# A fused layer pair on one core: half 0's choice moved behind the index scores, rotary products held for them, and only a quarter of the input rows prepared ahead of attention

## What is computed

```python
x = x + attention(layernorm(x))     # top-32 index mask, rotary Q and K
x = x + mixture0(layernorm(x))      # rms_norm, 8 experts, top 2
x = x + state_space(layernorm(x))
x = mixture1(layernorm(x)) + x      # 8 experts, top 2, and a shared one
```

```python
index_scores = sum_h relu(iq_h @ ik) * iw_h          # 4 heads
mask = top-32 of index_scores in each row
attn = softmax(rope(Q) @ rope(K) * scale + mask) @ V
...
scores = rms_norm(x) @ w_router
ids = top_k(scores, 2); c = softmax(scores)[ids]
out = sum over the 2 chosen experts of c * expert(x)
```

## Time and profile before

| | us |
|---|---|
| three runs | 1346.49 to 1353.12, median 1350.16 |
| the profiled execution | 1351.29 |
| its span in the trace | 1349.5 |
| VectorE busy in it | 945.9 (70%) |
| TensorE busy in it | 1057.1 (78%) |
| start until ScalarE's first normalised tile | 16.47 |
| attention | 16.47 to 251.3 |
| first expert tile on TensorE | 285.74 |

### The profile page before, as it was taken

The page is one execution under the profiler, slowest core; times in us unless marked ns, Lnnn a source line. Parts: engine busy times, 40 slices in busy tenths (PEclk is TensorE's granted clock), DMA queues, the critical chain, the costliest instruction groups (busy, mean ns, idle before and its releaser), DMA issues. The chain is left out here.

```text
span 1349.5 us, 20293 instructions
## 1 busy us (share of the span) xinstructions
PE 1057.1 (78%) x4202; PEld 615.6 (46%) x4203; DVE 945.9 (70%) x2283; ACT 746.9 (55%) x1826; POOL 834.6 (62%) x602
## 2 busy tenths in 40 slices
PE   3888867449999955888989888897784229999995
PEld 3666745327777831333333333333223215555563
DVE  4999899633333333799999999989997715455573
ACT  3767746235555547858586776756531115555542
POOL 1433248447517557877886888788782577437276
PEclk9999879569999976999999999899898559999998
DMA  8994002226524425343434354443540026435335
GB/s 244 160 148 138 1 8 24 18 35 88 81 57 88 85 33 111 86 143 131 156 115 169 124 157 124 135 160 115 184 143 0 32 57 94 83 74 95 79 67 103
DMA packets 140460, 133.22 MB, mean 99 GB/s; under 512 B 14579, under 2 KB 121699, under 8 KB 140259
## 3 DMA queue, kind: packets, MB, share of 16 engines
q1 hardware_dynamic: 107106, 115.55, 32.2%
q0 software_dynamic: 33280, 16.86, 11.2%
HBM read 98.66 MB, written 31.60 MB: 97 GB/s over the span
## 5 line engine op out<-in xcount | busy, mean ns | idle before, releaser
L1740 POOL TENSOR_TENSOR ss_HC<-ss_Hs,ss_Cb 128x512 f32<-128x512 f32 x256 | 317.6, 1270 | 91.7 <-PE ss_Y L1514 70.7
L1514 PE MATMUL ss_Y<-ss_HC,g_ident 128*128 128x512 f32 x512 | 267.8, 641 | 46.4 <-POOL ss_HC L1740 38.8
L1809 DVE TENSOR_TENSOR_SCAN ss_Hs<-ss_dA,ss_dBu 128x512 f32<-128x512 f32 x256 | 297.2, 1203 | 6.3 <-ACT ss_dA L1656 6.0
L827 POOL DMA_INDIRECT rows<-m_XS,g_slot x128 | 181.3, 1417 | 69.2 <-issue 35.8
L1127 PE MATMUL m_x_UP<-g_m_w,m_x_gT 128*128 (+1 forms) x532 | 204.5, 491 | 6.7 <-issue 2.6
L1656 ACT ACTIVATE ss_dA<-ss_delta,g_A 128x510 f32<-128x510 f32 x256 | 167.7, 712 | 56.9 <-DVE ss_Hs L1809 56.7
L1514 PEld LDWEIGHTS ss_Y<-ss_HC,g_ident 128*128 128x128 f32 x512 | 90.2, 197 | 207.1 <-POOL ss_HC L1740 148.1
L1801 DVE TENSOR_TENSOR ss_dBu<-ss_duP,ss_Bb 128x512 f32<-128x512 f32 x256 | 163.4, 685 | 21.0 <-DMA ss_Bb<-bc_rows 16.7
L1147 PEld LDWEIGHTS m_x_DP<-g_m_w,m_x_hT 128*128 128x128 f32 (+1 forms) x908 | 131.5, 190 | 80.0 <-issue 38.3
L1147 PE MATMUL m_x_DP<-g_m_w,m_x_hT 128*128 (+3 forms) x908 | 161.7, 296 | 5.3 <-ACT m_x_hT L1214 3.1
L1107 POOL DMA_INDIRECT g_X<-out_rows,g_slot x64 | 99.3, 1551 | 80.1 <-DMA out_rows<-m_x_YO 57.5
(11 more groups left out here) (266 smaller groups left out, 1826.5 us busy)
## 6 DMA issues: line engine op xcount, KB each, us to landing
ss_Bb<-bc_rows SPq DMA_DIRECT2D x64, 512.0 KB, 4.9
ss_Cb<-bc_rows SPq DMA_DIRECT2D x64, 512.0 KB, 4.0
rows<-g_Z SPq DMA_DIRECT2D x2, 5031.0 KB, 55.3
m_x_G<-rows SPq DMA_DIRECT2D x156, 64.5 KB
out_rows<-m_x_YO SPq DMA_DIRECT2D x156, 64.0 KB
g_m_w<-in_w_up SPq DMA_DIRECT2D x1, 2816.0 KB, 10.2
g_m_b<-in_b SPq DMA_DIRECT2D x1, 2160.0 KB, 11.5
g_X<-in_x SPq DMA_DIRECT2D x4, 512.0 KB, 5.7
```

The lines of the kernel that those rows point to most:

```text
L827: self.nc.gpsimd.indirect_dma_start(self.XG, bass.IndirectOffsetOnAxis(self.rt.slot[k][:, t:t + 1], 0), self.XS[:, t, :], None, compute_op ...
L1514: ins = nc.tensor.matmul(Yp[:, h, :], ident[:], HC[n % 2][:, h, :], start=False, stop=n == N - 1)
L1740: nc.gpsimd.tensor_tensor(HC[n % 2][:, h, :], Hs[n % 4][:, h, :], Cb[g % 2][:, n % 2, :], ALU.mult).then_inc(hc_ready.sem, 1)
L1809: v_.tensor_tensor_scan(Hs[n % 4][:, h, :], dA[n % NA][:, h, :, :].rearrange("p s t -> p (s t)"), dBu[:, h, :], 0.0, ALU.mult, ALU.add).th ...
```

## The change

1. *Input rows.* `InputRows` takes the place of `row_stats`. Ahead of attention only the first quarter (8 tiles) gets moments and scales, and the constants are loaded right behind the first quarter of X. The other 24 tiles' moments open VectorE's program in attention, their root is in ScalarE's step 0, their scales at the end of VectorE's step 1. ScalarE's normalising for sequence 4 waits for them.
2. *Statistics for the mixture.* BN_STATS of the updated tiles stands behind round 1 of `choose`, the variance behind round 2, and the `Chain` wait after the statistics goes.
3. *Step 12.* `vector_choose` stands behind index scores, round 0 and update; round 1 and 2 follow, then `vector_slots`, then round 3. `vector_tables` goes to the experts' block, first on VectorE; TensorE waits for it there.
4. *GpSimd from step 12 on.* The bias addition of sequence s (and so the rotary products behind it in GpSimd's program) waits for the index scores of s-1.
5. *Second choice.* The reweighting and the first 4 of its 16 scatters stand at the end of GpSimd's program in attention; 12 stay in the experts' block.

```diff
-def row_stats(nc, tag, chain, shifted, rooted, X, mean, scales, eps2, loads=None, x_loaded=(), shift=None):
+class InputRows:
...
+    def vector_moments(self, dve, lo, hi):
+        v, link = self.nc.vector, Chain(dve, self.chain)
+        n = T // len(self.loaded)
+        for t in range(lo, hi):
+            if t % n == 0:
+                dve.wait_ge(self.loaded[t // n], 16)
+            ins = v.bn_stats(self.st[:, t, :], self.X[:, t * D:(t + 1) * D])
...
+def first_rows(nc, rows, hi, loads):
...
+            rows.vector_moments(dve, 0, hi)
+            rows.vector_scales(dve, 0, 0, hi)
...
                 def normalise(s, v):
+                    if s == early // 2:
+                        act.wait_ge(rows.scaled.sem, rows.scaled.after(1))
...
+                    if s == 0:
+                        rows.scalar_root(act, 1, early, T)
...
                     u = 1 - v
-                    if s == LAST:
-                        dve.wait_ge(d.s.scalar_kept.sem, d.s.scalar_kept.after(1))
-                        d.vector_choose(dve, 0)
                     if middle:
                         index_scores(s - 1, u)
                         choose(s - 1, u, range(0, 1))
                     if tail and s >= 3:
                         update(s - 3, u)
-                        if s - 3 < HT // 2:
-                            dve.wait_ge(x_updated.sem, x_updated.after(s - 3))
-                            d.vector_stats(dve, 2 * (s - 3), 2 * (s - 2))
-                        if s - 3 in (GS - 1, 2 * GS - 1):
-                            b = (s - 3) // GS
-                            d.vector_variance(dve, b * d.G, (b + 1) * d.G)
+                    if s == LAST:
+                        dve.wait_ge(d.s.scalar_kept.sem, d.s.scalar_kept.after(1))
+                        d.vector_choose(dve, 0)
                     if middle:
                         choose(s - 1, u, range(1, 2))
+                    if 3 <= s < 3 + HT // 2:
+                        dve.wait_ge(x_updated.sem, x_updated.after(s - 3))
+                        d.vector_stats(dve, 2 * (s - 3), 2 * (s - 2))
+                    if middle:
+                        choose(s - 1, u, range(2, 3))
+                    if s - 3 in (GS - 1, 2 * GS - 1):
+                        b = (s - 3) // GS
+                        d.vector_variance(dve, GS * (b + 1) - 1, b * d.G, (b + 1) * d.G)
                     if s == LAST:
                         d.vector_slots(dve, 0)
-                        d.vector_tables(dve, 0)
                     if middle:
-                        choose(s - 1, u, range(2, TOPK // 8))
+                        choose(s - 1, u, range(3, TOPK // 8))
+                    if s == 1:
+                        rows.vector_scales(dve, 1, early, T)
...
+                rows.vector_moments(dve, early, T)
                 steps(dve, step)
...
+                        if s >= LAST:
+                            pool.wait_ge(idx.sem, idx.after(s - 1))
+                            pool.sem_inc(skipped, 1)
                         x = X[:, ds(s * W2, W2)].rearrange("p (t d) -> p t d", d=D)
...
                 steps(pool, step)
+                d.pool_reweight(pool, 0, 1)
+                d.pool_scatter(pool, 1, 0, HT // 4, ALU.add)
...
-        Chain(dve, self.chain)(ins)
+        ins.then_inc(self.s.stated.sem, 1)
...
                 if inside:
-                    d.pool_reweight(pool, 0, 1)
-                    d.pool_scatter(pool, 1, 0, HT, ALU.add)
+                    d.pool_scatter(pool, 1, HT // 4, HT, ALU.add)
...
                         d.tensor_score(pe, d.HG + g, g * d.G)
+                    pe.wait_ge(d.s.tabled.sem, d.s.tabled.after(0))
...
                 if inside:
+                    d.vector_tables(dve, 0)
                     d.vector_stats(dve, HT, T)
...
             def first_loads(sp):
-                n = T // len(x_loaded)
-                for t in range(0, T, n):
-                    sp.dma_start(X[:, t * D:(t + n) * D].rearrange("p (t d) -> p t d", d=D), xd[:, t:t + n, :]).then_inc(x_loaded[t // n], 16)
-                for dst, src in first:
-                    sp.dma_start(dst, src).then_inc(first_loaded.sem, 16)
+                for q in range(len(rows.loaded)):
+                    sp.dma_start(X[:, q * early * D:(q + 1) * early * D].rearrange("p (t d) -> p t d", d=D),
+                                 xd[:, q * early:(q + 1) * early, :]).then_inc(rows.loaded[q], 16)
+                    if q == 0:
+                        for dst, src in first:
+                            sp.dma_start(dst, src).then_inc(first_loaded.sem, 16)
```

More of the change, by code:

```diff
@@ L139, in attention, with _ @@
+def first_rows(nc, rows, hi, loads):
+    with nc.Block() as block:
+        @block.sync
+        def _(sp):
+            loads(sp)
+        @block.vector
+        def _(dve):
+            rows.vector_moments(dve, 0, hi)
+            rows.vector_scales(dve, 0, 0, hi)
+        @block.scalar
+        def _(act):
+            rows.scalar_root(act, 0, 0, hi)
+def attention(nc, rows, early, d, zeroed, X, shift, scales, ident, w, bias, b_iw, b_o, rope, loads, clear):
     with ExitStack() as ctx:
@@ L1909, in later_loads @@
                     sp.dma_start(dst, src).then_inc(w1.loaded.sem, 16)
[L1911 removed]
+            first_rows(nc, rows, early, first_loads)
             wait_loaded(nc, first_loaded, len(first))
[L1913 removed]
+            attention(nc, rows, early, d0, zeroed, X, shift, scales, ident, w, bias, b_iw, b_o, rope, later_loads, clear)
         experts(nc, "m0_x_", tile_signals, d0, True, X, XS0, rt, XG0, Y0, None, HT, w0, True, ident)
```

86 lines of the change are left out of this document (35 added, 51 removed).

## The result

The changed kernel takes 1329.97 us (median of 4 runs, 1327.85 to 1335.7) against 1351.43 of the kernel before (1346.49 to 1353.12): ratio 0.9854, 95% interval 0.9813 to 0.9895. I had said 1326, within 1319 to 1336. The profiled execution has a span of 1327.7 against 1349.5 us, 21.8 less.

The account below looks back on a forecast made before the run. VectorE was taken to bound attention, GpSimd's second-choice scatters the gap behind it, then TensorE the expert stage. 4.0 + 3.3 + 3.0 + 6.7 + 7.5 = 24.5 off 1351.3 gave 1326.8, stated as 1326, range 1319 to 1336.

Parts of the forecast that it names:

- The start, 4.0: Ahead of attention: starting with 8 tiles' statistics gains 5.4 us, less 1.4 for six scales in step 1: 4.0.
- The statistics, 3.3: Updated tiles' statistics in attention: 7 x 0.35 us from their new place plus 0.8 for the two variances: 3.3.
- Step 12, 3.0: Attention step 12: 1.9 us from waits, 1.2 from tables, 3.1 from blocking, less 3.2 for the choice blocked: 3.0.
- the 6.2: Upper figure for step 12's gain in us, if nothing blocks the choice, as the scans suggested.
- Steps 13 to 15, 6.7: Attention steps 13 to 15: held GpSimd work leaves the index scores, 7.2 us less 0.5 for a relu wait: 6.7.
- Second choice, 7.5: Gap before the first expert tile: four scatters and the copy's wait leave it, 8.0 us less 0.3 and 0.2: 7.5.
- The sum: Whole kernel: the five terms together take 24.5 us off the profiled execution's 1351.3, giving 1326.8.
- the choice isn't blocked: Rival for step 12: GpSimd does not block the choice, 3.2 us more gain, 1323; chance 0.12.
- Another engine becomes the bound: Rival in attention: TensorE's and ScalarE's round takes half of 3.3 + 3.0 + 6.7, 1333; chance 0.12.
- The moved scatters come late: Rival at attention's end: scatters stretch or GpSimd still scatters when VectorE is through; 7.5 shrinks to about 1, 1333; chance 0.05.
- The start: Rival ahead of attention: SyncE's issue or barrier takes as long, or moments reach into at_IW; 4.0 lost, 1330; chance 0.06.
- slower, by the clock: Rival in the expert stage: 125 us of it at granted clock 0.80 instead of 1.00, ending above 1357; chance 0.03.

Follow-up runs that it names:

- d_start_back: Changed kernel with all 32 tiles' statistics and scales, and all of X loaded, ahead of attention again; at_IW of step 1 at 38.01 against 33.31 us.
- a4_hold_rotary: Changed kernel with GpSimd's rotary product of step 12 held until the choice has weighed; at_IW of step 12 22.88 us behind step 11's instead of 24.86.
- e_best: Changed kernel with step 12's rotary product held, bias additions of steps 14 and 15 in GpSimd's wait, five scatters moved instead of four; 1323.65 us, ratio 0.9805.
- a1_no_hold: Changed kernel without GpSimd's wait for the index scores ahead of the bias addition from step 12 on; 1325.91 us.
- c_old_place_free: Changed kernel without GpSimd's hold and with slots and tables where they stood before; 1326.41 us.
- b_scatters_back: Changed kernel with the copy and all 16 scatters of the second choice in the experts' block; first scatter to first tile 89.05 us.
- e_change_again: The changed kernel itself, unaltered, measured and profiled a second time; 1329.46 us.

## Why the prediction was right, and where its steps were not

- **The start, 4.0:** 4.66 measured, and d_start_back gives it back. Attention started 0.66 earlier than I put it, since SyncE was through at 9.60 and not at 10.4. Of the spare time that I put at 3.8 us, 1.94 went to the wait for X and 1.3 to the stretched TENSOR_SCALAR, which my sum left out; 0.56 remained.
- **The statistics, 3.3:** 2.80 by step 11 in the profile, 2.27 in the second. In the plain step 0.40 each (11.43 against 11.83) instead of 0.35, which made 3.41 by step 9. Step 10 gave nothing: VectorE waits 1.03 for ScalarE's root in it, as I feared, and it took 18.35 us against 17.74. It took 16.13 to 18.41 in the kernels that are the same up to there, so the term's size is known only within 2 us.
- **Step 12, 3.0:** 3.89 measured (24.86 us against 28.75). The mechanism was right and its price near: 2.32 - 0.29 + 1.00 - 0.29 = 2.74 for the 3.2 that I took. The waits gave 2.4 (3.23 less 0.87) instead of 1.9. The Trainium skill ("SBUF — State Buffer", section "Who interferes with whom") gave that side of the bound, and here the trace agrees. The other side, that nothing is blocked, rested on a misreading: the scans of the earlier trace rows do not read two SBUF tensors. ss_dBu, their second input, lies in PSUM in this kernel, so they say nothing against the rule, and the 6.2 had no row behind it. The one scan that does read two SBUF tensors beside GpSimd, in a4_hold_rotary and e_best, was slowed (0.86 instead of 0.41).
- **Steps 13 to 15, 6.7: this step failed.** The words were "Held GpSimd work leaves them". The scores did become 2.46 everywhere, but the hold has no part in it (a1_no_hold). The slots' new place has one: without it and without the hold the scores of steps 13 and 14 lose 1.8 us again. The other 5.4 of the 7.2 are gone without either (c_old_place_free), and what freed them stays open. I priced the hold and did not work out where GpSimd's scatters would stand. Nor did all 7.2 us reach the first tile. By at_IW of step 15 4.95 more us had been gained since step 12 (16.30 against 11.35), and 6.59 in the second profile, whose step 15 was not lengthened by the lower clock (last section). From there to its end in attention VectorE takes longer than before (20.21 us against 18.67), so that 3.41 are left of the 6.7, and 5.37 in the second profile.
- **Second choice, 7.5:** 7.74 from the opening of the block to the first tile (26.37 against 34.11), and 5.6 to 7.0 by b_scatters_back, which counts the later opening too. I had said GpSimd's last scatter and VectorE's end would be within 1 us. VectorE ended 2.36 us behind its end, and yet the block waited for GpSimd: 3.54 us pass there behind the last scatter, which no row of before shows, since GpSimd had long been idle at that change of block.
- **The sum:** 24.5 became 22.25 at the first tile and 21.8 in the span. VectorE's end fell from 251.32 to 236.56; before, and then in the second profile of the change:

```profile
250.71 0.61 DVE L452 SCALAR_TENSOR_TENSOR g_X<-at_b,at_rinv,g_X 128x128 f32<-128x128 f32 x2 [3.83 <-PE at_b L308]
251.63 3.19 DVE L646 BATCH_NORM_STATS2 m_d_st<-g_X 128x6 f32<-128x128 f32 x16 [0.32 <-PEq L214]
```

```profile
237.43 0.47 DVE L828 TENSOR_TENSOR m_d_cmp<-m_d_end,g_tile_of_half 1x312 f32<-1x312 f32 x1 [1.41 <-PEq L223]
```

These 14.76 us are 4.66 + 2.80 + 3.89 + 3.41, where I had 4.0 + 3.3 + 3.0 + 6.7 = 17.0. At the change of block 0.24 are lost to GpSimd (idle 0.56 instead of 0.32), and 1.1 in the second profile; then come the 7.74. So the total came within 10% partly by luck: the start and step 12 gave 1.6 more than I put, steps 13 to 15 3.3 less. And GpSimd took over by no more than 0.2 to 1.1 us; the kernel with six scatters shows that the terms don't add beyond that. The last part passed one to one, within the 5 us by which that stretch varies anyway. The range's lower end was wrong by its own terms: 1326.8 less 3.2, 1.6 and 1.1 is 1320.9, not 1319.
- **The rivals:** "the choice isn't blocked" fell by the 2.32 and 1.00 us rows. "Another engine becomes the bound" was half true, with GpSimd in the place of TensorE and ScalarE. "The moved scatters come late" was nearest in its mechanism; its price was 0.24 us in the first profile and 1.1 in the second. Whether the 0.2 us by which the scatter of the earlier trace rows is longer are the lockout that the prediction saw in them, no run tells. "The start" fell by the 4.66, and "slower, by the clock" by the third window: the expert stage ran at 1.00 again, and the rest took 1064.2 us against 1063.8.

## What to carry to other kernels

When a bound engine is relieved, work out the whole schedule of the engine that feeds the next stage, from its first instruction on and over the change of block, and compare its end with the relieved engine's: the terms of a sum count only as far as the later of the two. A wait that is put in to keep two engines apart should be tested by leaving it out, since an edit beside it may have moved them apart already. Before a row is taken as a counterexample, look where its operands lie: the scans that seemed to go unblocked read one input from PSUM. And where an effect is smaller than the scatter of the times, compare marks in the traces at several places: what is there before the edit's place is not the edit's.

## What the runs showed of the hardware that I had not expected

- Where GpSimd ends a block with scatters, its next instruction comes 3.43 to 3.68 us behind the last one's end (in all twelve profiles with this order), while inside a block the next scatter follows in 0.30.
- A VectorE TENSOR_TENSOR with two tensors in SBUF that starts 0.30 us behind GpSimd's rotary product (2.48 us) takes 2.32 us, to within 0.14 us of its end; MAX8 and MATCH_REPLACE8 beside a rotary product keep their 0.74 and 0.41 us (200.62 and 201.34 in the changed kernel), and TENSOR_REDUCE beside the addition its 0.29. A TENSOR_TENSOR_SCAN of 128x128 with both inputs in SBUF took 0.86 instead of 0.41 beside the addition; the scans of the earlier trace rows, with one input in PSUM, kept their 1.20.
- TensorE's granted clock differed between two executions of the changed kernel in the same stretch, 0.89 and 1.00 (columns as in the first windows, the first profile above, e_change_again below), and with it step 15's 8 projections, 3.67 and 1.99 us:

```profile
205.00:220.00 15.00, 12.84 (x70) 10.18 (x69) 12.46 (x47) 10.13 (x25) 12.37 (x9) 0.89 0.27 22
...
208.05 3.67 PE L246 MATMUL at_b<-at_xT,a_w 128*128 128x256 f32 x8 [1.64 <-ACT at_xT L344]
```

```profile
205.00:220.00 15.00, 12.22 (x74) 9.27 (x70) 14.11 (x52) 11.78 (x30) 13.40 (x10) 1.00 0.27 22
...
208.29 1.99 PE L246 MATMUL at_b<-at_xT,a_w 128*128 128x256 f32 x8 [1.64 <-ACT at_xT L344]
```
